# A GAT pass on one core: fewer hand-overs between TensorE and VectorE in each window, and ScalarE's staging copies spread over two steps

## The reference

```
x = (h @ W).reshape(n, H, C)                      # H = 4
e = leaky_relu(a_src[src] + a_dst[dst], 0.2)
m = segment_max(e, dst)
e = exp(e - m[dst])
denom = segment_sum(e, dst)
alpha = e / denom[dst]
out = segment_sum(x[src] * alpha, dst)
```

## Time and profile before

| | us |
|---|---|
| median of three runs | 6411.62 (6409.93 to 6416.7) |
| profiled execution, its own time | 6413.51 |
| its span in the trace | 6411.5 |
| the stage of the change, first product to last | 2318 to about 3700 |
| one window in it | about 45 |

### The profile page before, as it was taken

How to read it: one execution, slowest core, us unless ns; L and a number is a source line. 1 busy time by engine, 2 the same in 40 slices (tenths; PEclk the granted TensorE clock), 3 DMA queues, 4 the chain that set the end, 5 groups by cost and what they waited for, 6 DMA issues and landing times. The chain is left out here.

```text
span 6411.5 us, 101358 instructions
## 1 busy us (share of the span) xinstructions
PE 3480.2 (54%) x16378; PEld 2938.9 (46%) x16379; DVE 2933.9 (46%) x7516; ACT 2034.7 (32%) x7274; POOL 3910.4 (61%) x4083
## 2 busy tenths in 40 slices
PE   0645555455556357777777748534455555333332
PEld 0544555444555346656665646423444443333331
DVE  4333344344556556666666654533444453222221
ACT  0111111111222135555555533135566652111110
POOL 1777776777777576655554100477777704777776
PEclk9767778766677568999899979666667777555555
DMA  3222222211111223222222120122222204444443
GB/s 102 60 62 63 63 65 63 70 53 53 53 52 53 45 74 93 87 88 87 83 84 79 58 92 0 30 53 53 54 53 54 53 23 135 131 131 131 131 132 110
DMA packets 401376, 474.12 MB, mean 74 GB/s; under 512 B 95282, under 2 KB 295150, under 8 KB 401167
## 3 DMA queue, kind: packets, MB, share of 16 engines
q0 software_dynamic: 130464, 264.37, 15.5%
q1 hardware_dynamic: 144287, 146.87, 7.3%
q10 hardware_dynamic: 126528, 61.89, 3.2%
HBM read 315.65 MB, written 157.15 MB: 74 GB/s over the span
## 5 line engine op out<-in xcount | busy, mean ns | idle before, releaser
L1396 PE MATMUL pa<-arena,weighted 128*128 x4480 | 865.3, 368 | 826.9 <-POOLq L1189 489.6
L1396 PEld LDWEIGHTS pa<-arena,weighted 128*128 128x128 f32 x4480 | 799.3, 274 | 882.1 <-issue 881.8
L1677 POOL DMA_INDIRECT arena<-t_tab,src_idx x784 | 789.6, 1007 | 552.0 <-issue 206.1
L596 POOL DMA_INDIRECT arena<-y_tab,slot x784 | 739.7, 943 | 456.9 <-ACT slot L688 247.6
L1195 POOL DMA_INDIRECT arena<-h_tab,src_idx x784 | 740.2, 944 | 363.7 <-issue 219.7
L1195 POOL DMA_INDIRECT arena<-sage_tab,src_idx x784 | 739.7, 944 | 262.4 <-issue 218.2
L2409 POOL DMA_INDIRECT arena<-t_tab,src_idx x784 | 744.2, 949 | 245.0 <-issue 225.8
L645 DVE TENSOR_TENSOR_SCAN scan_t<-mask,scan_t,pa 128x512 f32<-128x512 bf16 x196 | 250.8, 1280 | 736.6 <-PE pa L669 736.6
L2713 ACT ACTIVATE weighted<-arena,weighted 128x64 f32 x2240 | 552.0, 334 | 19.2
L669 PE MATMUL pa<-ident,arena 128*128 128x128 f32 x784 | 218.3, 434 | 603.7 <-DMA arena<-y_tab,slot 603.7
L2631 PE MATMUL pa<-weighted 128*128 128x130 f32 x2240 | 452.4, 379 | 144.7 <-ACT weighted L2713 130.8
(11 more groups left out here) (526 smaller groups left out, 6722.3 us busy)
## 6 DMA issues: line engine op xcount, KB each, us to landing
gat_tab<-out_rows SPq DMA_DIRECT2D x248, 260.0 KB
scan_rows<-out_rows ACTq DMA_DIRECT2D x196, 256.0 KB, 3.7
arena<-t_tab,src_idx POOLq DMA_INDIRECT x1568
mask<-cut_row SPq DMA_DIRECT2D x196, 128.0 KB, 3.1
arena<-gat_tab SPq DMA_DIRECT2D x7, 1820.0 KB, 7.2
arena<-h_tab,src_idx POOLq DMA_INDIRECT x784
arena<-sage_tab,src_idx POOLq DMA_INDIRECT x784
y_tab<-arena SPq DMA_DIRECT2D x49, 256.0 KB, 2.3
```

Of the source, the lines that this page charges most:

```text
L596: nc.gpsimd.indirect_dma_start(out=rows(c, t), out_offset=None, in_=table[:, :], in_offset=bass.IndirectOffsetOnAxis(ap=slot[:, c, t:t + 1 ...
L1396: ins = nc.tensor.matmul(pa[:, b * CE:b * CE + RW], hot[b][:, t * P:(t + 1) * P], ring[:, bass.ds(start + t * RW, RW)], start=(t == 0), st ...
L1677: nc.gpsimd.indirect_dma_start(out=rows[:, g % QR * QT + t, :], out_offset=None, in_=t1_tab[:, :], in_offset=bass.IndirectOffsetOnAxis(ap= ...
```

## The change

Two parts of one pass change; what is computed stays the same.

First, the hand-over of a window. VectorE makes the forward scan and the backward scan of each tile at once, ahead of the exchange between tiles (`run` now has three operations on 128 columns: a copy and two scans). TensorE turns the last and the first column together (`ends_out`), VectorE makes both scans over the 32 tiles in one go (`link`, one partition, in step 4), TensorE turns both results back together (`ends_back`), and `top` spreads them (a copy and two scans). `carries`, `firsts_up`, `chain` and `rise` are gone as hand-overs of their own: of six waits of TensorE for the hand-over, four remain. Each stands ahead of a step's products, for what VectorE did in the step before: `turn` ahead of step 3, `ends_out` ahead of 4, `ends_back` ahead of 5, `tops_back` ahead of 6. VectorE does its parts behind `build` and `weigh` of the same step, where `run` stood ahead of them. `factor` moves ahead of the add in step 0, and the number of the tile is loaded at the head of the window.

Second, ScalarE's staging. The copy of the flags (`stage_flags`) and the wait for the next window's groups stand behind its step 0; the eight copies stand among the activations of steps 1 and 2, one ahead of each tile's pair.

```diff
-                    v.tensor_tensor_scan(run1, cut1, own_ps1, -BIG, ALU.add, ALU.max).then_inc(window_run.sem, 1)
+                    step(v.tensor_tensor_scan(run1, cut1, own_ps1, -BIG, ALU.add, ALU.max))
+                    v.tensor_tensor_scan(backwards(whole1[:, 0:P - 1]), backwards(cut_ps1[:, 1:P]), backwards(run1[:, 0:P - 1]),
+                                         run1[:, P - 1:P], ALU.add, ALU.max).then_inc(window_run.sem, 1)
...
+                def link(w, step, tile):
                     back = of_fine(dve, w, QW + 2, 0, QK)
                     v.tensor_copy(here1, tile_row1[:, :, bass.ds(tile, QK)])
                     step(v.tensor_copy(chain1[:, 0, :], link1[:, bass.ds(back, 1), :].rearrange("o t h -> o (t h)")))
                     after(dve, window_lasts, w + 1)
                     for hd in range(H1):
+                        v.tensor_tensor_scan(backwards(ahead1[:, 0:QK, hd]), backwards(here1[:, 1, :]), backwards(firsts_ps1[:, :, hd]),
+                                             -BIG, ALU.add, ALU.max)
+                    for hd in range(H1):
                         ins = v.tensor_tensor_scan(chain1[:, 1:QK + 1, hd], here1[:, 0, :], lasts_ps1[:, :, hd],
                                                    chain1[:, 0, hd:hd + 1], ALU.add, ALU.max)
-                    ins.then_inc(window_chained.sem, 1)
-
-                def rise(w, step):
...
+                    step(ins)
+                    v.tensor_tensor(link1, ahead1, chain1, ALU.max)
+                    step(v.tensor_tensor(tie1[:, 0:QK, :], ahead1[:, 1:QK + 1, :],
+                                         here1[:, 2, :].unsqueeze(2).broadcast_to([1, QK, H1]), ALU.add))
+                    v.tensor_tensor(tie1[:, 0:QK, :], tie1[:, 0:QK, :], chain1[:, 1:QK + 1, :], ALU.max).then_inc(window_linked.sem, 1)
...
-                    step(v.tensor_tensor(tops1[:, P - 1:P], raised1[:, P - 1:P], tie_ps1, ALU.max))
+                    step(v.tensor_copy(tops1[:, P - 1:P + 1], ends_ps1))
+                    step(v.tensor_tensor_scan(raised1[:, 0:P - 1], cut1[:, 0:P - 1], whole1[:, 0:P - 1], tops1[:, P:P + 1], ALU.add, ALU.max))
...
                     for q in range(QW):
-                        if next_here and q == 3:
-                            tile = of_fine(dve, w + 1, QW, 0, ET)
-                            run(w + 1, steps)
                         if here:
                             build(w * QW + q, q % 2)
                             weigh(w * QW + q, q % 2)
+                            if q == 0:
+                                factor(w)
                         if next_here:
+                            if q == 3:
+                                run(w + 1, steps)
                             if q == 4:
-                                rise(w + 1, steps)
+                                link(w + 1, steps, tile)
...
+                    ahead = {3: turn, 4: ends_out, 5: ends_back, 6: tops_back} if next_here else {}
                     for q in range(QW):
-                        if next_here and q == 3:
-                            turn(w + 1)
-                            lasts(w + 1)
...
+                        if q in ahead:
+                            ahead[q](w + 1)
...
                     for q in range(QW):
-                        if next_here and q == 2:
-                            stage_window(w + 1)
+                        staged = [(q - 1) * QT + t for t in range(QT)] if next_here and q in (1, 2) else []
                         if here:
-                            weigh(w, q)
+                            weigh(w, q, dict(enumerate(staged)))
...
+                        if next_here and q == 0:
+                            stage_flags(w + 1)
```

More of the change, by code:

```diff
@@ L1931, in body @@
                     if next_here:
-                        steps = window_step.of(dve, w + 1, 10)
+                        steps = window_step.of(dve, w + 1, 11)
+                        tile = of_fine(dve, w + 1, QW, 0, ET)
                     for q in range(QW):
-                        if next_here and q == 3:
-                            tile = of_fine(dve, w + 1, QW, 0, ET)
-                            run(w + 1, steps)
                         if here:
@@ L1952, in body @@
                                     add(w - 1, QW - 1)
-                                factor(w)
                             else:
                                 add(w, q - 1)
-                        if next_here:
-                            if q == 3:
-                                chain(w + 1, steps, tile)
-                            if q == 4:
-                                link(w + 1, steps)
                 blocks_f = scratch[:, 560:560 + QS]
@@ L1976, in _ @@
                 v.memset(link1, -BIG)
-                v.memset(tie1, -BIG)
+                v.memset(ahead1, -BIG / 16)
                 spread_starts()
@@ L2102, in stage_window, with stage_rows, weigh @@
                                    cut_tiles1[:, bass.ds(tile, QK)].unsqueeze(2).broadcast_to([P, QK, H1]))
+                    need = of_fine(act, w, QW + 1, 1, QN)
                     wait_apart(act, group_landed.sem, group_landed.past(need))
-                    for k in range(QW):
-                        start = of_fine(act, w, k, 0, (QR - 1) * QT * TW)
-                        ins = nc.scalar.copy(seen1[:, k * QT * H1:(k + 1) * QT * H1].rearrange("p (t h) -> p t h", h=H1),
-                                             ring1[:, bass.ds(start, QT * TW)].rearrange("p (t c) -> p t c", c=TW)[:, :, D:TW])
-                    ins.then_inc(window_staged.sem, 1)
-                def weigh(w, q):
+                def stage_rows(w, k):
+                    start = of_fine(act, w, k, 0, (QR - 1) * QT * TW)
+                    ins = nc.scalar.copy(seen1[:, k * QT * H1:(k + 1) * QT * H1].rearrange("p (t h) -> p t h", h=H1),
+                                         ring1[:, bass.ds(start, QT * TW)].rearrange("p (t c) -> p t c", c=TW)[:, :, D:TW])
+                    if k == QW - 1:
+                        ins.then_inc(window_staged.sem, 1)
+                def weigh(w, q, stage):
                     s, b = w * QW + q, q % 2
@@ L2121, in weigh @@
                     for t in range(QT):
+                        if t in stage:
+                            stage_rows(w + 1, stage[t])
                         for hd in range(2, H1):
@@ L2137, in body @@
                     for q in range(QW):
-                        if next_here and q == 2:
-                            stage_window(w + 1)
+                        staged = [(q - 1) * QT + t for t in range(QT)] if next_here and q in (1, 2) else []
                         if here:
-                            weigh(w, q)
+                            weigh(w, q, dict(enumerate(staged)))
+                        else:
+                            for k in staged:
+                                stage_rows(w + 1, k)
+                        if next_here and q == 0:
+                            stage_flags(w + 1)
                     if next_here:
```

46 lines of the change are left out of this document (17 added, 29 removed).

## The result

The changed kernel takes 6168.69 us (median of four, 6167.85 to 6173.04) against 6412.47 for the kernel before; the ratio is 0.9621 with a 95% interval of 0.9604 to 0.9637. It is 243.8 us faster; 6140 was forecast, which is 28.7 less than what was measured. The profiled execution has a span of 6171.0.

A forecast was written before the change was run, and what follows sets the result against it. No engine is full: 45.1 us windows are bound by waits between engines and TensorE's slow clock. Twenty windows of 34.3 and ten of 38 save 287, less 15 for joints: 272 off 6411.6 gives 6140, range 6095 to 6265.

The forecast's parts named there:

- the sum: One window on TensorE: 28 us of products plus each remaining wait and transpose, 34.3 against 45.1 before.
- 1.0 and 1.3 for ScalarE: TensorE's waits ahead of steps 1 and 2 for ScalarE's spread staging, replacing 3.96 and its slow clock of 2.8.
- some 2 us: In the kernel before, TensorE's loss per window to transposes and the start of products behind a wait.
- The bound of 1.3 for a load that nothing covers: ScalarE's upper case: each load waits for the activations, so a staged tile takes 1.3 us, a step 5.6 to 6.0.
- Rival C: ScalarE's loads in steps 1 and 2 are not covered: windows of 39.5 us, 6243 to 6260; chance 0.12.
- Rivals A and B: TensorE's clock: A, it stays slow, 6270 (0.13); B, slow enough to lose, 6560 with four steps at half clock (0.03).
- The rule on short idle pieces: Short idle pieces between TensorE's groups of matmuls make the clock swing; by it, rival A's 6270 would be the forecast.
- 1.23 gained: TensorE's wait ahead of `rescale` in step 0 goes when `factor` moves ahead of the add; 0.3 stay for the product.
- 38 for the first ten windows: GpSimd's gathers bind the first third: 28.7 a window at 1.30 is 37 us, taken as 38 with ring losses.
- Rival D: GpSimd's gathers slow to 1.45 us each, as shorter windows put stores and gathers closer together: 6200; chance 0.10.
- joints that no row shows: Allowance of 0.5 us a window, 15 in all, taken off the gain of 287 to leave 272.
- The lower end of the range: Gathers overlap well, joints cost nothing, waits of steps 1 and 5 halve: 30 x 32.8 with ten at 36, 6085 to 6100.

The follow-up runs named there:

- e12: Changed kernel without the eight register loads of ScalarE's staging (copies from fixed columns of another table, so wrong scores): 6121.62 us, ratio 0.9545.
- e2: Changed kernel with ScalarE's staging put back in one block ahead of step 2, hand-over and `factor` as changed: 6293.05 us, ratio 0.9814.
- e3: Changed kernel with `factor` back behind the add of step 0, so the rescaling product waits for step 7's sums: 6169.36 us, ratio 0.9620.

## Why the prediction held, and by which step it was off

**The waits.** Step by step, the sum had 4.5, 4.8, 3.75, 4.15, 4.9, 3.7, 4.7, 3.8 for steps 0 to 7; the trace has 4.94, 5.23, 3.83, 4.14, 5.19, 3.69, 4.95, 3.98. The waits themselves were right: 1.0 and 1.3 for ScalarE came as 1.12 and 1.46, 1.1 and 1.2 for VectorE as 1.21 and 1.22, and 0.2 ahead of step 4 as 0.24. **The term that was too small** is the start of products behind a wait, which the account of the kernel before lumped into "some 2 us" and the sum counted only for the transposes. From 2969.09 to 2974.32 are 5.23 us; 3.5 are products and 1.46 idle time, and 0.27 are left. With four such waits it is 1.1 us a window, and the waits' own excess is 0.5: 35.9 instead of 34.3, 33 us over twenty windows. Two of VectorE's prices were off without harm: behind `link` stands 0.16 of idle time instead of the 0.35 for its wait on itself, and `link` took 2.4 instead of 2.3.

**ScalarE.** The 0.84 for a staged tile, the 4.3 to the end of a step and the 5.0 to the next came as 0.85, 4.31 and 5.06 in step 1, the last as 5.31 in step 2. The bound of 1.3 for a load that nothing covers was wrong in kind: behind a queued pair it is partly covered, and e12 shows 0.16 a tile plus what it delays at the step's ends. Rival C falls.

**The clock.** Waits of 1.1 to 1.5, four in a window, left the granted clock at 1.00 in all late windows of the changed kernel. In its first ten it was low behind every wait ahead of step 1, down to those of 2.4 to 2.6. With the block of staging alone put back (e2) it was 0.50 behind the wait of 5.17. Rivals A and B, which had the slow clock in every window, fall. The rule on short idle pieces from the Trainium skill that the prediction weighed (TensorE: Matmul & The Clock Gate, A second HAM failure mode: psum-queue depth-cycling) has no instance in the late windows; the trace does not agree with it for waits of 1.1 to 1.5.

**`factor`.** The prediction priced its move at 1.23 gained and the wait of step 1 at 1.0 lost, each for itself. The sum was right and the two terms were one: e3 shows that either wait stands for the other. Moving `factor` is worth nothing that can be measured in this kernel (6169.36 and 6168.69).

**The gathers.** The forecast had 38 for the first ten windows, and they are 39.4, 14 us over ten. The place of the loss was named, ScalarE's wait for the next groups ahead of its step 1, but not its second half: the granted clock falls behind every one of these waits. What was too low is the count of gathers. The 28.7 a window came from the stretch from 2400 on, behind the two densest windows; over all ten the trace has 29.7, which at 1.30 are 38.6 and not 37. The windows follow it: the six with a wait of 2.4 to 2.6 are 37.2 to 37.4 long and have 28 gathers, windows 1, 2 and 4 are 44.6, 41.2 and 42.0 long and have 35, 31 and 32. Whether the slow clock adds to that isn't shown. Rival D's 1.45 a gather did not come: 646.8 busy and 179.3 of issue for 636 are 1.30.

**The joints.** The 15 us left for "joints that no row shows" stood for the first of these terms. 287 less 33 less 14 is 240; measured are 243.8. So the measured time lies 29 behind the forecast because the terms of 33 and 14 stand against an allowance of 15, with some 3 the other way (the stage took 1355.4 before, not 1353).

**The lower end of the range.** Its sum doesn't come out. With the waits of steps 1 and 5 at half, a window is 33.2 and not 32.8, and twenty windows of 32.8 with ten of 36 are 6075, not 6085 to 6100. No other term rests on it.

## What to carry to other kernels

Where several engines run in step, write the window anew as one timeline: an idle stretch that goes at one place can come back at the next place whose own chain is later, and terms that are priced one by one can be counted twice. Here a block of small operations behind register loads cost its full length ahead of a wait, and less when it was cut up among queued work: the loads still cost 2.1 us a window, because in the staged steps the sequencer's own time is longer than the activations'. When such a stage is shortened, ask for the supply next, and count it for the densest windows, not for the mean.

## What the runs showed of the hardware that was not expected

A product that starts behind a wait costs TensorE about 0.27 us more than the idle time that the trace shows, at full clock (0.22 to 0.27 ahead of steps 1, 2 and 7). Part of this is how the profile draws a product: each is recorded 0.38 long, while they start 0.22 apart. ScalarE takes 0.71 for a register load with its copy; eight loads in a window cost 47 us in the whole even among activations (e12). In the changed kernel the granted clock stayed at 1.00 behind waits of 1.1 to 1.5 and fell behind every wait of 2.4 and more. A wait of 1.2 us on TensorE could be put in or taken out without any measurable change of the time (e3).
